# Products of ones in two of TensorE's waits ahead of the last batch's values

## The reference

```
q = layernorm(x) @ w_q ;  k, v = ctx @ w_kv
x = x + tanh(g_xattn) * (softmax(q k^T / 8) v @ w_out + b_out)
```

```
probs = softmax(layernorm(x) @ Wr^T) ; top 2, weights normalised to sum 1
x = x + tanh(g_ffn) * sum over the two: weight * (silu(xn @ W1_e^T) @ W2_e^T)
```

## Time and profile before

| | |
|---|---|
| median of 3 runs | 532.32 us (531.59 to 533.25) |
| profiled execution | 530.12 us, span 528.4 us |
| TensorE products | 482.2 us busy (91%), 6630 |
| VectorE, ScalarE, GpSimd | 69%, 70%, 70% busy |
| mean granted clock of TensorE | 0.982 of full speed |

### The profile page before, as it was taken

One profiled execution on the slowest core, in us unless ns is written; L12 is line 12 of the kernel. 1 busy time (PEld: TensorE's weight loads), 2 busy tenths in 40 slices (PEclk: granted clock), 3 DMA queues, 4 the chain that ended last, 5 costly groups with the idle time before them and its releaser, 6 DMA issues. The chain is left out here.

```text
span 528.4 us, 17570 instructions
## 1 busy us (share of the span) xinstructions
PE 482.2 (91%) x6630; PEld 431.7 (82%) x6630; DVE 364.0 (69%) x866; ACT 371.4 (70%) x577; POOL 369.7 (70%) x414
## 2 busy tenths in 40 slices
PE   2889699999999999999776999898999999999994
PEld 2877578888897888888556899888999999999993
DVE  5799899899989989898996757544344443444431
ACT  1888989999899998988764577544555655546551
POOL 5469779798999999899988566546554645545432
PEclk9999989999999999999897999999999999999998
DMA  7953415163261626335174648877888888888712
GB/s 288 398 197 117 146 55 188 51 208 117 91 223 46 229 63 192 115 105 198 39 252 142 211 126 293 253 198 210 257 223 251 235 232 263 218 244 245 211 23 30
DMA packets 35060, 94.86 MB, mean 180 GB/s; under 512 B 4507, under 2 KB 24475, under 8 KB 27645
## 3 DMA queue, kind: packets, MB, share of 16 engines
q1 hardware_dynamic: 25812, 82.79, 45.7%
q0 software_dynamic: 8592, 10.81, 11.4%
q10 hardware_dynamic: 576, 0.14, 0.1%
HBM read 74.45 MB, written 19.28 MB: 177 GB/s over the span
## 5 line engine op out<-in xcount | busy, mean ns | idle before, releaser
L1541 DVE SCALAR_TENSOR_TENSOR hT<-hf,h_scale,hT 128x512 f16<-128x512 f32 x78 | 58.3, 750 | 86.1 <-ACT hT L1016 86.1
L1707 PE MATMUL st_bank<-xsT,w_tile 128*128 128x128 f16 x1872 | 113.9, 222 | 1.3 <-DVE xsT L1535 1.3
L1707 PEld LDWEIGHTS st_bank<-xsT,w_tile 128*128 128x128 f16 x1872 | 110.1, 99 | 2.1 <-DVE xsT L1535 1.6
L730 POOL DMA_INDIRECT out<-yt,row_of x39 | 62.4, 1600 | 61.8 <-DVE yt L1550 49.0
L1010 ACT ACTIVATE hf<-st_bank,z_scale 128x512 f32<-128x512 f32 x78 | 52.9, 678 | 44.6 <-PE st_bank L1707 38.6
L618 POOL TENSOR_TENSOR pT<-pT 120x512 f16<-120x512 f32 x64 | 77.3, 1223 | 6.1 <-ACT pT L884 5.9
L1707 PE MATMUL o_bank<-w2s,hT 128*128 x600 | 69.7, 273 | 0.3 <-DVE yt L1550 0.3
L1016 ACT ACTIVATE hT<-hf,h_scale 128x512 f16<-128x512 f32 x78 | 56.3, 722 | 10.6 <-PE o_bank L1707 4.3
L1707 PEld LDWEIGHTS o_bank<-w2s,hT 128*128 128x128 f16 x600 | 57.4, 98 | 7.3 <-issue 0.8
L883 ACT ACTIVATE pT<-st_bank,exp_bias,logit_scale 120x512 f32<-120x512 f32 x64 | 50.0, 781 | 14.9 <-PE st_bank L1924 14.4
L663 POOL TENSOR_SCALAR stage<-stage,upw 128x512 f32<-128x512 f32 x32 | 56.6, 1769 | 4.1 <-ACT w_hi L983 4.1
(11 more groups left out here) (224 smaller groups left out, 1008.3 us busy)
## 6 DMA issues: line engine op xcount, KB each, us to landing
w_tile<-w_split SPq DMA_DIRECT2D x39, 1024.0 KB, 5.9
stage<-in_w SPq DMA_DIRECT2D x16, 1024.0 KB, 5.0
w_split<-w_hi SPq DMA_DIRECT2D x8, 512.0 KB, 2.8
w_split<-stage SPq DMA_DIRECT2D x8, 512.0 KB, 3.9
out<-x SPq DMA_DIRECT2D x17, 128.0 KB
xin<-in_x SPq DMA_DIRECT2D x8, 256.0 KB
w2s<-in_wkv SPq DMA_DIRECT2D x2, 1024.0 KB, 12.0
xres<-in_x SPq DMA_DIRECT2D x16, 128.0 KB, 2.1
```

The source lines that it names most:

```text
L730: pool.indirect_dma_start(out=out[0:rows], out_offset=bass.IndirectOffsetOnAxis(row_of[:, t:t + 1], 0), in_=yt[t % XG][:], in_offset=None, ...
L1541: nc.vector.scalar_tensor_tensor(out=hT[par][:, 1, 4 * a:4 * a + 4, :], in0=hf[par][:, 512 * a:512 * a + 512].rearrange("p (c n) -> p c n" ...
L1707: ins = pe.matmul(out, lhs[i](a), rhs[i](c), start=(i == 0 and a + c == 0), stop=(i == n - 1 and a == 1))
```

## The change

`spare(name, b, n)` does nothing except for the last batch; there it waits for the bank that `name` will use, and runs n products of a 128 x 128 matrix of ones with itself into it. Nobody reads them: the transposes of `OT1a` overwrite the bank later. It is called ahead of `values(7, 1, 1)` with 18 and ahead of `values(7, 2, 0)` with 44.

```diff
+            def spare(name, b, n):
+                if b != B - 1:
+                    return
+                dst = bank_free(name, b)
+                for _ in range(n):
+                    pe.matmul(dst[:, 0:P], onesb[:], onesb[:], start=True, stop=True)
...
                 attn_maxima(p + 3, 0)
+                spare("OT1a", p + 1, 18)
                 values(p + 1, 1, 1)
...
                 tile_T(p, 4)
+                spare("OT1a", p + 1, 44)
                 values(p + 1, 2, 0)
```

## The result

| | before | changed |
|---|---|---|
| median | 531.57 us (21 runs, 527.89 to 533.99) | 528.19 us (21 runs, 525.45 to 532.37) |
| ratio | | 0.9944, 95% interval 0.9925 to 0.9963 |
| profiled execution | 530.12 us, span 528.4 | 530.40 us, span 528.7 |

The change makes the kernel 3.0 us faster by the ratio (0.0056 x 531.6). The profiled executions alone say nothing of it: the changed one took 0.3 us longer. They have to be read stretch by stretch.

The account below looks back on a forecast made before the run. TensorE was taken to bound the kernel, its clock falling behind a 2.80 us wait. Added 0, given back 2.3 us; allowing for shorter falls, gain 1.7: 532.3 - 1.7 = 530.6 us, range 529.4 to 533.0.

Parts of the forecast that it names:

- What bounds the kernel: Whole kernel: TensorE is busy 91% of the span, and from 341.63 us the last chain is its expert tiles alone.
- the waits: Last batch: TensorE waits 1.35 us before 280.23 and 2.80 us before 285.16; the clock reads 0.50 behind the second.
- the price of a product: Both fill groups: 60 ns per product of ones, so 1.08 us and 2.64 us, both hidden in the waits.
- The 84 ns row: 40 early products of ones from 12.56 us take 3.36 us; at that price the groups end 0.3 and 0.7 late.
- What the fill gives: From 285.16 us to the values of unit 3: at full clock TensorE is there 2.8 us sooner.
- what is late next: Values of unit 3: they wait for GpSimd's low halves and go at 290.84, which leaves 2.3 us.
- such a case: A timed execution with a 3.4 us fall behind the second wait: 1.2 us lost, 0.8 to gain.
- Down to the end: From unit 3's values to 341.6 us: GpSimd's and TensorE's chains come forward together, carrying the 2.3 us through.
- The wait for the gather near 339: Sign in the changed profile: TensorE's wait for tile 9's gathered rows should still be about 1.7 us.
- the first rival: Gather at 335.41 to 341.59: a later wait, grown to 4.0 us, eats the gain; 532.3 us, chance 0.12.
- my own list of costs: Last batch only: 18 and 44 products, 62 weight loads, two semaphore waits; nothing removed or moved, no DMA.
- The sum: Whole kernel: 0 added, 2.3 us given back; gain 0.8 to 2.3, taken as 1.7, so 530.6 us.

Follow-up runs that it names:

- changed kernel again: The changed kernel run once more without edit, beside the kernel before: 528.27 us, ratio 0.9962.
- only44: The changed kernel without the 18 products, keeping the 44 ahead of the values of unit 2: 526.70 us, ratio 0.9951 to the kernel before.
- turns_before: gather_before with VectorE's four small add_turns operations moved behind the low half of tile 10's rows, no fills: 526.82 us, ratio 0.9908 to the kernel before.
- shift128: The kernel before with 128 more products of ones at its very start: 528.67 us, ratio 0.9968.
- fill_shift66: The changed kernel with 66 more products of ones at its start, 128 added in all: 527.67 us, ratio 0.9945 to the kernel before.
- gather_before: The kernel before with GpSimd's gather of tile 9 issued ahead of the read of the table, no fills: 527.45 us, ratio 0.9931.
- gather_after: The changed kernel with the gather of tile 9 issued ahead of the read of the table: 527.45 us, ratio 0.9935 to the kernel before.
- turns_after: gather_after with VectorE's four small add_turns operations moved behind the low half of tile 10's rows: 525.95 us, ratio 0.9904 to the kernel before.
- only18: The changed kernel without the 44 products, keeping the 18 ahead of the values of unit 1: 528.96 us, ratio 0.9978 to the kernel before.
- half22: The changed kernel with 22 instead of 44 products in the second wait: 527.13 us, ratio 0.9942 to the kernel before.

## Why the prediction was wrong

**What bounds the kernel, the waits, the price of a product: right.** The 44 products took 56 ns each where I had taken 60. In the changed kernel again and in only44 they end inside their wait, and the values of unit 2 start 9.07 to 9.08 us after A, as before. In the first profile, behind the fall at 261, the wait was shorter and the 44 ran to its end and beyond: the values start at A + 8.31, against A + 7.99 in turns_before, 0.3 us late. Nothing came of it, as both reach V at A + 15.33. The 84 ns row that I had set against the 60 was no price of its own: in the trace these products start 106 ns apart up to 14.5 us and 56 ns apart from there on.

The Trainium skill's 81 ns ("TensorE: Matmul & The Clock Gate", "Back-to-back issue gap") does not hold for these products: 44 of them took 2.46 us (284.40 to 286.86).

**What the fill gives, and what is late next: right to 0.1 us.** I had 17.03 - 2.3 = 14.7 us from A to V, with the wait for GpSimd's low halves inside; nine of the ten profiles with 44 or 22 products show 14.72 or 14.73. The clock fell in all seven profiles in which the wait of 2.8 us stands open, and in none of the ten with products in it; the eighth without them, turns_before, had the shorter wait and no fall. The fall is 3.4 us long in five of the seven and then costs 1.2 us; the text had allowed for such a case (0.8).

**Down to the end: this step failed.** It said: "The wait for the gather near 339 should still be about 1.7 us; if it has grown to 4, the first rival is right." It neither stayed nor grew; it went. I had held TensorE's and GpSimd's chains to move together and asked only whether a fixed stretch of DMA could take the gain back. The part that I overlooked stands two lines into my own list of costs: "nothing is removed or moved, and no DMA". 62 products with their weight loads are 124 more instructions, and instructions come by DMA, in packets of 16 KB. The page of before has 56 of them in q8, beside 6630 products and as many weight loads, the page of the changed kernel 57:

```profile
q8 instruction: 56, 0.92, 0.7%
```

That 256 instructions make one packet is borne out by shift128 and fill_shift66, where 128 products with 128 weight loads bring the packets back to their places; so 124 move them by about half a period. In the kernel before, one starts at V + 35.9, 2.2 us ahead of the end of the table's DMA (331.22, V + 38.1). Between the two kernels run again, the read of the table starts 1.3 us later where the packet lies there, and the gather behind it is issued 1.1 us later, beside a 1 MB weight transfer issued at V + 42.3; it then takes 6.2 to 6.3 us instead of 5.1 at the most.

The Trainium skill ("TensorE: Matmul & The Clock Gate", "Step-by-step: what each phase is for") speaks of the 64-byte instruction of a product, and by an estimate from that figure 16 KB hold the same 256.

The wait is worth 2.3 us in the profiles (48.5 against 46.3), and up to 4.1 where a fall follows it (V + 66.8 against V + 62.7 at tile 10). Removed by itself it gives 3.2 to 3.7 us (gather_before), which is the size of the change's whole gain, or more.

**The sum.** I took 1.7 us for the clock and 0 for the gather, from a base of 532.32 us, the median of three runs. Over 21 runs the base is 531.57, so 0.8 of the 2.4 us between 530.6 and 528.19 is the base and not the mechanism. Measured for the fills in timed executions, each against the same kernel without them: 0 (gather_after against gather_before), 0.2 (turns_after against turns_before), 1.4 (only44 against only18) and 1.2 us (fill_shift66 against shift128, where the gather's wait stands in both profiles). The parts do not add up. With the wait gone the fills give next to nothing; with the wait back (fill_shift66) the gain is still 2.9 us. So I can't divide the 3.0 us: the wait's going is enough to give them, but it is not shown that the changed kernel owes them to it.

One likely reason why the clock gives less in the time than in its stretch is that falls came elsewhere: one of 6.8 us between 253 and 269 in three profiles (changed, changed again, turns_before), where before has one of 3.4, and others at 343 to 360, behind the waits for tile 9's and tile 10's rows, in five of the 13 profiles that leave VectorE's four operations where they were, and in none of the five that move them. The mean granted clock of whole executions is 0.988 both before and changed. But in the three pairs that differ by fills alone and have the same start it is higher with them: 0.992 (only44) against 0.989 (only18), 0.990 against 0.988 (the earlier gather), 0.994 against 0.991 (turns). That is 1 to 3 us less at the low clock, no difference more than about twice its standard error. Whether the fills only exchange one fall for another, or it was chance in these executions, is not settled.

**What is shown and what is inferred.** Shown: 62 products far from the last batch give the gain and take the wait away; the earlier gather gives it too; 128 bring the late read and the wait back, and with them about half of the time (ratio 0.9968 against 0.9936, the intervals overlap); the fetch's place and the read of the table go together in 17 of 18 profiles. Inferred: that the fetch's packet itself holds up the table's last packets; no view shows one packet behind another. Why fill_shift66 is as fast as the changed kernel in spite of its wait is open.

## What to carry to other kernels

A change that adds instructions to a long unrolled program moves the fetches of all that follow, so test it against the same number of instructions in a harmless place before you believe its mechanism. When a kernel's end hangs on one gather that is issued in the last moment, issue it earlier: a microsecond of luck in the DMA queues then costs nothing, and here it gave by itself as much as the whole change. And with a fill, look first where the wait is in each pass, and wait for the bank only where products follow.

## What the runs showed of the hardware

- Instruction fetch shares the DMA engines with data and can be seen: the page's queue q8 moves 16 KB packets, 56 for 6630 products and 6630 weight loads, and 256 more of these bring the packets near the last batch back to their places. The Trainium skill, "DMA: Bandwidth & Descriptors", "Queues, rings and completion order", lists refill in a row of queues that is the runtime's own; the profiles here show instruction packets in q8 and q14.
- A wait of 2.8 us after little work was followed by the low clock (0.50) in seven of seven profiles. A wait of 1.97 us there was not, in the one profile that has it (turns_before), nor were the 1.57 us that 22 products left open (half22). The falls last 3.4 or 6.8 us and cost 1.2 and 2.3 us of the stretch.
- Twenty and more executions of the kernel before, or of the changed one, spread over 5 to 7 us (before: 527.9 to 534.0), so a single profiled execution cannot show a gain of 3 us by its total.
